# A sequence mixer on one core: state products padded to all 128 rows, projection weight streamed in pieces, norms from one function table, outputs with 128 tokens

## The reference, cut to what matters

```
x = x + mixer(layernorm(x))
x = x + cross_attention(layernorm(x), ctx)
x = x + moe(layernorm(x))
```

```
bc = (value @ W_bc.T).reshape(B, T, 32, 4, 32)        # Bz, Bx, Cz, Cx: 32 states a head
bc = bc / (sqrt(sum(bc*bc, -1)) + 1e-8)
z = S * (z - dt*A*s + dt*Bz*u)                        # per head, state and head channel, step by step
s = s + dt*z + dt*Bx*u
y = Cz . z + Cx . s
out = ((y + skip*value) * silu(gate)) @ W_out.T
```

## Time and profile before

| | |
|---|---|
| median of 3 runs | 3144.58 us (3139.78 to 3146.74) |
| span of the profiled execution | 3057.5 us |
| what lies around the span (median less span) | 87.1 us |
| TensorE busy in the span | 2816.9 us, 92% |
| VectorE busy | 2063.0 us, 67% |
| ScalarE busy | 1286.8 us, 42% |
| DMA | 366.15 MB, mean 120 GB/s |
| 13 units of the mixer, 508.85 to 1899.47 us | 1390.62 us, 106.97 us each |

### The profile page before, as it was taken

One profiled execution on the slowest core, in us unless ns is written; L12 is line 12 of the kernel. 1 busy time (PEld: TensorE's weight loads), 2 busy tenths in 40 slices (PEclk: granted clock), 3 DMA queues, 4 the chain that ended last, 5 costly groups with the idle time before them and its releaser, 6 DMA issues. The chain is left out here.

```text
span 3057.5 us, 83082 instructions
## 1 busy us (share of the span) xinstructions
PE 2816.9 (92%) x34208; PEld 2144.9 (70%) x34208; DVE 2063.0 (67%) x7110; ACT 1286.8 (42%) x2244; POOL 286.6 (9%) x227
## 2 busy tenths in 40 slices
PE   7965999999999999999999999589879999999998
PEld 3434778778877887787788878533335667888887
DVE  7658999999999999898999999555656201111111
ACT  4634545554454554455455545133324222333332
POOL 0000000000000000000000000000000661333344
PEclk9977999999999999999999999779988999999999
DMA  7874354254435424433542542210006332777776
GB/s 270 233 204 113 80 126 108 64 126 112 102 73 129 108 70 116 112 91 83 124 108 58 135 112 76 69 42 1 1 1 253 109 120 87 197 201 197 197 200 181
DMA packets 249233, 366.15 MB, mean 120 GB/s; under 512 B 57771, under 2 KB 172092, under 8 KB 238140
## 3 DMA queue, kind: packets, MB, share of 16 engines
q1 hardware_dynamic: 226428, 335.99, 39.9%
q0 software_dynamic: 22464, 25.31, 3.9%
HBM read 264.99 MB, written 99.84 MB: 119 GB/s over the span
## 5 line engine op out<-in xcount | busy, mean ns | idle before, releaser
L671 PE MATMUL ring<-valt,wbc 128*128 128x256 f32 x4096 | 947.9, 388 | 31.8 <-DMA valt<-valt_scratch 27.7
L671 PEld LDWEIGHTS ring<-valt,wbc 128*128 128x128 f32 x4096 | 777.4, 194 | 169.0 <-issue 61.5
L824 ACT COPY bc<-ring 128x512 f32<-128x512 f32 x256 | 149.5, 584 | 736.4 <-PE ring L671 736.4
L984 DVE TENSOR_TENSOR uu<-phi,coef 128x64 f32<-128x64 f32 x2048 | 355.1, 211 | 2.1
L990 DVE TENSOR_TENSOR phi<-phi,uu 128x64 f32<-128x64 f32 x2048 | 354.5, 211 | 0.1
L2101 DVE TENSOR_SCALAR f_yr<-fp_y,f_meta 128x256 f32<-128x256 f32 x124 | 54.3, 479 | 423.1 <-PE fp_y L1918 423.1
L729 PE MATMUL yp<-bc,hpad 32*32 32x64 f32 x8192 | 260.2, 289 | 5.0 <-DVE hc L1092 5.0
L729 PEld LDWEIGHTS yp<-bc,hpad 32*32 32x32 f32 x8192 | 225.5, 122 | 50.7 <-issue 50.6
L1985 ACT ACTIVATE f_hT<-fp_h,f_b 128x256 f32<-128x256 f32 x248 | 117.4, 473 | 327.3 <-PE fp_h L1909 327.3
L1918 PE MATMUL fp_y<-f_w,f_hT 128*128 128x256 f32 x992 | 230.7, 386 | 7.9
L1909 PE MATMUL fp_h<-f_xrt,f_w 128*128 128x256 f32 x992 | 225.9, 381 | 0.9 <-ACT f_xrt L1974 0.9
(11 more groups left out here) (227 smaller groups left out, 4006.1 us busy)
## 6 DMA issues: line engine op xcount, KB each, us to landing
f_w<-in_W_dram SPq DMA_DIRECT2D x128, 512.0 KB, 4.2
coef<-par_scratch SPq DMA_DIRECT2D x128, 256.0 KB
fb<-fac_scratch SPq DMA_DIRECT2D x256, 128.0 KB, 3.4
fc<-fac_scratch SPq DMA_DIRECT2D x256, 128.0 KB, 3.8
xg_scratch<-f_fill SPq DMA_DIRECT2D x16, 1032.0 KB, 17.5
f_xr<-xg_scratch SPq DMA_DIRECT2D x64, 258.0 KB, 4.9
vtok_scratch<-p_vtok SPq DMA_DIRECT2D x32, 512.0 KB, 7.9
dub<-vtok_scratch SPq DMA_DIRECT2D x16, 1024.0 KB, 7.3
```

Of the source, the lines that this page charges most:

```text
L671: mm = pe.matmul(ring[:, p % 2, v * UT:(v + 1) * UT], wbc[:, k, g, first + v, :], valt[:, u % 2, k, :], start=(k == 0), stop=(k == 3))
L824: nc.scalar.copy(bc[:, gp, first:first + 2, i // 2, :], o).then_inc(bc_ready, 1)
L984: made[k] = mark(V.tensor_tensor(uu[:, k].rearrange("p i (g b) -> p i g b", b=B), phi[:, t, ::-1, k, :].rearrange("p i (g b) -> p i g b", ...
```

## The change

Five edits, all in the mixer and its weight.

1. **State products.** `hpad` becomes an operand with all 128 rows for each j: ScalarE writes it four times (once for each j), scaled by a mask `own` that leaves only head j's 32 rows. `mixed_states` takes all 128 rows of both operands; its outputs stay 32 columns each at the same place of `yp`.
2. **Weight.** `wbc` (64 KB a partition) is gone. A ring `wring` of 4 pieces of 512 KB (a piece is what one `projected` call needs) takes its place. Four pieces are loaded at the start; after that, ScalarE's queue issues the next load into a slot right after the square (L827) that frees it: 252 loads of 512 KB, 16 in a unit, where one load of 8 MB stood.
3. **Norms.** The square root becomes Exp(0.5 Ln(x + 1e-30)), so that each call of `norms` has two Ln and two Exp and no Sqrt; a function table with both is loaded once ahead of the mixer's work.
4. **Outputs.** `outputs` takes 128 tokens at once: the half loop r is gone, 8 products of 128 x 128 with 256 moving columns where there were 16 of 128 x 64. Tokens of `xs` stand in another order, so `load_x` and `store_x` have 4 DMAs of 32 partitions instead of 2 of 64.
5. One more constant (`own`) is loaded, and one tile (`tiny`) is set.

```diff
-            sp.dma_start(wbc[:], d["W_bc"].rearrange("(k p) (g c o) -> p k g c o", p=P, g=G, c=4)).then_inc(wbc_in, 16)
+            for p in range(WRING):
+                sp.dma_start(wring[:, p], d["W_bc"][p]).then_inc(wbc_in, 16)
...
+WPIECES = 4 * GP
+WRING = 4
...
-        hpad = sb("hpad", [P, 2, 2, B, 2 * DH])
+        hpad = sb("hpad", [P, J, DH + 4 * B * 2 * DH])
+        own = sb("own", [P, J])
...
             def store_x(u):
                 sp.wait_ge(x1_ready, u + 1)
-                for r in range(2):
-                    sp.dma_start(x1v[u, r], xs[L * r:L * r + L]).then_inc(x_out, 16)
+                for b in range(B):
+                    sp.dma_start(x1v[u, b], xs[b::B]).then_inc(x_out, 16)
...
             def projected(u, gp, i):                       # TensorE
+                if p >= WRING:
+                    pe.wait_ge(piece_in[p % WRING], 16 * (p // WRING))
...
-                        mm = pe.matmul(ring[:, p % 2, v * UT:(v + 1) * UT], wbc[:, k, g, first + v, :], valt[:, u % 2, k, :],
+                        mm = pe.matmul(ring[:, p % 2, v * UT:(v + 1) * UT], wring[:, p % WRING, k, v, :], valt[:, u % 2, k, :],
...
             def mixed_states(u, gp, more, un, gn):
-                pe.wait_ge(hpad_ready, 2 * n + 2)
+                pe.wait_ge(hpad_ready, J * n + J)
...
+                            k = DH * (2 * ((2 * v + i) * B + b) + 1 - i)
                             for j in range(J):
-                                r = slice(N * j, N * j + N)
-                                pe.matmul(yp[r, b * L:(b + 1) * L], hpad[r, v, i, b, :],
-                                          turns(bc[r, gp, 2 + v, i, :])[:, :, b],
+                                pe.matmul(yp[N * j:N * j + N, b * L:(b + 1) * L], hpad[:, j, k:k + 2 * DH],
+                                          turns(bc[:, gp, 2 + v, i, :])[:, :, b],
...
                 for q in range(2):
-                    for r in range(2):
-                        for k in range(4):
-                            mm = pe.matmul(yp[L * r:L * r + L, q * DM:(q + 1) * DM],
-                                           turns(sg[:, k, :])[:, :, 2 * q + r], wout[:, k, :],
+                    for k in range(4):
+                        mm = pe.matmul(yp[:, q * DM:(q + 1) * DM], sg[:, k, q * P:(q + 1) * P], wout[:, k, :],
...
+            nc.scalar.preload_act_table_set("natural_log_exp_and_others")
...
             def projected(u, gp, i):                       # ScalarE
                 nc.scalar.activation(sq[:, p % 2], o, ACT.Square).then_inc(sq_ready, 1)
+                if p + WRING < WPIECES * NU:
+                    act.dma_start(wring[:, p % WRING], d["W_bc"][(p + WRING) % WPIECES]) \
+                        .then_inc(piece_in[p % WRING], 16)
...
-                nc.scalar.activation(nr[:], ssp[:, 0:UT], ACT.Sqrt).then_inc(nr_root, 1)
+                nc.scalar.activation(nr[:], ssp[:, 0:UT], ACT.Ln, bias=tiny[:, 0:1]).then_inc(nr_square, 1)
+                act.wait_ge(nr_square, n + 1)
+                nc.scalar.activation(nr[:], nr[:], ACT.Exp, scale=0.5).then_inc(nr_root, 1)
...
-                for i in range(2):
-                    nc.scalar.copy(hpad[:, :, i, :, i * DH:(i + 1) * DH], hc[:, gp, :, i]).then_inc(hpad_ready, 1)
+                h = hc[:, gp].rearrange("p v i b e -> p (v i b) e")
+                for j in range(J):
+                    nc.scalar.activation(hpad[:, j, DH:].rearrange("p (x e) -> p x e", e=2 * DH)[:, :, 0:DH], h,
+                                         ACT.Copy, scale=own[:, j:j + 1]).then_inc(hpad_ready, 1)
```

More of the change, by code:

```diff
@@ L28 @@
 EPS_LN, EPS_BC = 1e-5, 1e-8
+SMALLEST = 1e-30
 DT_MIN, DT_MAX, Y_MAX = 1e-4, 0.1, 0.106
@@ L48, in constants @@
     hn = jn[:, None] * G + np.arange(G)[None]
+    c["own"] = (jn[:, None] == np.arange(J)[None]).astype(np.float32)
     c["sel"] = (hn[:, :, None] == np.arange(H)[None, None]).astype(np.float32)
@@ L90, with projections @@
 PIDX = {k: i for i, k in enumerate(PRING)}
-def projections(nc, d, x, st, wbc):
+def projections(nc, d, x, st, wring):
     with ExitStack() as ctx:
@@ L198, in _ @@
             sp.wait_ge(raw_out, 32 * NPASS)
-            sp.wait_ge(wbc_in, 16)
+            sp.wait_ge(wbc_in, 16 * WRING)
         @block.tensor
@@ L401, with mixer @@
 UQ = NU // B
-def mixer(nc, d, st, wbc, x, x1):
+WPIECES = 4 * GP
+WRING = 4
+def mixer(nc, d, st, wring, x, x1):
     with ExitStack() as ctx:
@@ L425, in mixer @@
         epsb = sb("epsb", [P, 1])
+        tiny = sb("tiny", [P, 1])
         phi = sb("phi", [P, L + 1, 2, 2, LANES])
@@ L463, in mixer @@
         w_loaded = sem("w_loaded")
-        NW = 7
+        NW = 8
         set_ready = sem("set_ready")
@@ L481, in mixer @@
         sums_done = sem("sums_done")
+        piece_in = [sem(f"piece_in{i}") for i in range(WRING)]
+        nr_square = sem("nr_square")
         nr_root = sem("nr_root")
@@ L506, in turns @@
             return v.rearrange("p (t b) -> p t b", b=B)
-        xv = x.rearrange("(q r u s) m -> u r s q m", q=2, r=2, s=L)
-        x1v = x1.rearrange("(q r u s) m -> u r s q m", q=2, r=2, s=L)
+        xv = x.rearrange("(b u q t) m -> u b t q m", b=B, q=2, t=L // 2)
+        x1v = x1.rearrange("(b u q t) m -> u b t q m", b=B, q=2, t=L // 2)
         def par(u, q):
@@ L552, in load_x @@
             def load_x(u):
-                for r in range(2):
-                    sp.dma_start(xs[L * r:L * r + L], xv[u, r]).then_inc(x_in, 16)
+                for b in range(B):
+                    sp.dma_start(xs[b::B], xv[u, b]).then_inc(x_in, 16)
             def store_x(u):
                 sp.wait_ge(x1_ready, u + 1)
-                for r in range(2):
-                    sp.dma_start(x1v[u, r], xs[L * r:L * r + L]).then_inc(x_out, 16)
+                for b in range(B):
+                    sp.dma_start(x1v[u, b], xs[b::B]).then_inc(x_out, 16)
             def store_factors(n):
@@ L587, in _ @@
                     (nega[:], d["A_states"]), (sel[:], d["sel"]), (ident[:], d["ident"]), (causal[:], d["causal"]),
-                    (resetm[:], d["resetm"]), (skip[:], d["skip"]),
+                    (resetm[:], d["resetm"]), (skip[:], d["skip"]), (own[:], d["own"]),
                     (wout[:], d["W_out"].rearrange("(k p) o -> p k o", p=P))):
@@ L642, in _ @@
                 if u > 0:
-                    sp.wait_ge(x_out, 32 * u)
+                    sp.wait_ge(x_out, 16 * B * u)
                     load_x(u)
@@ L652, in _ @@
             store_x(NU - 1)
-            sp.wait_ge(x_out, 32 * NU)
+            sp.wait_ge(x_out, 16 * B * NU)
         @block.tensor
@@ L663, in projected @@
                 p = 4 * n + i
-                g, first = 2 * gp + i // 2, 2 * (i % 2)
                 if gp == 0 and i == 0:
                     pe.wait_ge(valt_in, 16 * (u + 1))
+                if p >= WRING:
+                    pe.wait_ge(piece_in[p % WRING], 16 * (p // WRING))
                 if p >= 2:
@@ L680, in summed @@
                 if half == 0 and n > 0:
-                    pe.wait_ge(nr_root, n)
+                    pe.wait_ge(nr_square, n)
                 for i in range(2):
@@ L755, in outputs @@
                 for q in range(2):
-                    for r in range(2):
-                        for k in range(4):
-                            mm = pe.matmul(yp[L * r:L * r + L, q * DM:(q + 1) * DM],
-                                           turns(sg[:, k, :])[:, :, 2 * q + r], wout[:, k, :],
-                                           start=(k == 0), stop=(k == 3), skip_group_check=True)
+                    for k in range(4):
+                        mm = pe.matmul(yp[:, q * DM:(q + 1) * DM], sg[:, k, q * P:(q + 1) * P], wout[:, k, :],
+                                       start=(k == 0), stop=(k == 3), skip_group_check=True)
                 mm.then_inc(o_full, 1)
@@ L926, in _ @@
             V.memset(hpad[:], 0.0)
+            V.memset(tiny[:], SMALLEST)
             V.memset(one[:], 1.0).then_inc(set_ready, 1)
@@ L1097, in residual @@
                 dve.wait_ge(o_full, u + 1)
-                dve.wait_ge(x_in, 32 * (u + 1))
+                dve.wait_ge(x_in, 16 * B * (u + 1))
                 V.tensor_tensor(xs[:], yp[:].rearrange("p (q m) -> p q m", q=2), xs[:], ALU.add).then_inc(x1_ready, 1)
@@ L1154, in attention @@
         ("valt", (NU, P, 4, UT), F32), ("par", (UQ, 5, P, UT), F32), ("fac", (NU * GP, P, UT), F32))}
-    with nc.sbuf_tensor("wbc", [P, 4, G, 4, P], F32) as wbc:
-        projections(nc, d, x, st, wbc)
-        mixer(nc, d, st, wbc, x, x1)
+    with nc.sbuf_tensor("wring", [P, WRING, 4, 2, P], F32) as wring:
+        projections(nc, d, x, st, wring)
+        mixer(nc, d, st, wring, x, x1)
 SK, DC = 77, 192
@@ L2129, in layouts @@
     w = np.asarray(inputs["L0_attn_W_bc"]).reshape(G, J, 4, N, DI)[..., chan]
-    r["W_bc"] = w.transpose(0, 2, 1, 3, 4).reshape(H * 4 * N, DI).T
+    w = w.transpose(0, 2, 1, 3, 4).reshape(WPIECES, 2, P, 4, P)
+    r["W_bc"] = w.transpose(0, 4, 3, 1, 2)
```

## The result

| | before | after |
|---|---|---|
| median, 4 runs each | 3142.76 us (3139.78 to 3146.74) | 3225.48 us (3218.91 to 3231.91) |
| ratio | | 1.025, 95% interval 1.0226 to 1.0275: slower |

The account below looks back on a forecast made before the run. VectorE was taken as the bound: 101.3 us of work a unit plus 5.6 of waits. Terms 15 x (5.4 - 5.6) = -3, +2, +0.5, -4, +0.9 gave -3.6, so 3141 us, range 3116 to 3188.

Parts of the forecast that it names:

- The streamed weight: Mixer: 16 pieces a unit share the DMA engines with the factors; two `fb` waits of 5.4 us together a unit.
- rival 2: Streamed weight makes the factors late, `fb` waits together above 6.0 us a unit: 3180 us (3151 to 3200), chance 0.27.
- First `fb` wait: VectorE's wait for reloaded factors ahead of `inputs(u,2)`: two pieces delay the load, 2.7 us a unit, upper bound 3.8.
- Second wait: VectorE's wait for `fb` of `inputs(u,3)`: 3.2 less 1.0 plus 0.5, so 2.7 us a unit, upper bound 4.4.
- The first recurrence: Mixer's start: two pieces meet the parameters' store ahead of VectorE's first recurrence step, +2 us (0 to 3.3).
- State products: TensorE in each group: padded products fall from 30.1 to 19.0 ns, 5.7 us a unit; lower bound nothing saved.
- Rival 3: Padded state products are no faster, so about 1.0 us a unit of late waits stays: +15, 3156 us, chance 0.06.
- outputs: TensorE's outputs in each unit: 16 instructions at 232 ns, from 4.87 to 3.7 us, 1.15 saved a unit.
- the last store: Mixer's end: the last store has two more DMA issues, +0.9 us.
- At the end: TensorE on the path: state products 1.4 us shorter each, last outputs 6.41 to about 4.9, together -4 us.
- Norms: ScalarE: table loads go, chain to the factors 2.9 us shorter, removing VectorE's 10.5 us of waits in 13 units.
- The frame: Profiled span lay 87.1 us below the runs' median; the sum is a difference on that execution, added to the median.

Follow-up runs that it names:

- e5_turned: The kernel after, with read_out's last two VectorE instructions writing in the order in which TensorE reads, so without a step: ratio 1.0293.
- e8_early_turned: e7_early with the turned write of e5_turned: 3137.53 us, ratio 0.9962 to the kernel before.
- e2_resident: The kernel after with the whole weight resident in SBUF and the state products of before: 3140.35 us, ratio 0.9985 to before.
- e11_after_oldstate: The kernel after, weight still streamed, with the state products of before: 3236.36 us, ratio 1.0265 to before.
- e3_stream_only: The kernel before with the weight streamed and nothing else changed: 3261.22 us, ratio 1.034.
- e7_early: e2_resident with factors(n0+3) scaled, stored and loaded earlier, and the first coefficient set and coefs(u+1) later: 3115.01 us, ratio 0.9898 to before.
- e10_before_early: The kernel before with only the order moves of e7_early, keeping its longer norms and old outputs: 3170.07 us, ratio 1.007.
- e4_half_pieces: The kernel after with half the bytes loaded for each streamed piece, as many transfers: 3168.75 us, ratio 1.0058 to before.
- e6_shifted: The kernel after with a ring of 8 pieces and none issued in a unit's first group: 3176.37 us, ratio 1.0082 to before.
- experiment 5: The kernel before, unchanged, profiled a second time: span 3154.1 us in an execution of 3155.91, against a span of 3057.5 in the first profile.

## Why the prediction was wrong

**The streamed weight** is the step that failed. That its pieces would meet the factors of `inputs(u,2)` was its mechanism, and rival 2 its case against itself, with a chance of 0.27. The price of a piece was right too: 1.63 us of all DMA engines forecast, 1.65 measured (23.5% of 1453.2 us for 207 pieces in the DMA view of after). The size of the waits was wrong, in these terms.
- First `fb` wait: 2.7 a unit (bound 3.8); measured 4.7. The sum put two pieces ahead of the `fb` load alone. But the store of the factors runs through the same crowd ahead of the load: it landed 3.8 us later than before in the mean (9.2 against 5.4), and the load added 1.1 (8.0 against 6.8). The trip to DRAM and back was priced on one of its two legs, and the cost was mostly on the other.
- Second wait: 2.7 (bound 4.4), a fall of 0.3; measured 4.6, a rise of 1.6. The forecast took 1.0 off because the store takes "3.5 us now". That row is one unit; the mean from store to load was 2.9 before and is 2.8 in after, so there was next to nothing to take off. The load leg rose by 1.4 (5.3 to 6.7), where the sum had 0.5: in the unit shown the next piece was issued at 1116.60, beside the load of 1115.40.
- `fc`: put at nothing without a reason; measured 0.8.
- The first recurrence: +2 us (bound 3.3). The wait went from 12.64 to 18.49, but VectorE came to it earlier, and the step itself began 2.5 us later than in the first profile of before and 3.9 later than in the second (243.81 and 242.42, against 246.35). This term was small and nearly right.

The measured waits are 10.4 us a unit (135.2 / 13), where the sum had 5.4 and its upper bound 8.2. Over 15 units the 5.0 us between them are 75 us, most of the 84 us by which the forecast missed.

Two readings of the prediction were wrong beside this. The rows name one coefficient set, that of 1042.08, ahead of the full stretch of 1046 to 1052; the second was issued only at 1059.13. And rival 2's own sum, 3144.6 with +39, +2, +0.5, -4 and +0.9, is 3183 and not 3180. Neither changes the outcome.

**State products**: the bound "nothing saved" was the truth. 19.0 ns came from `mixed_values`, which reads without a step; the text named the step and set it aside because `causal_products` reads with it at 18.0. `e5_turned` and `e8_early_turned` show that the step costs these products half their time in either shape: 32.4 and 31.9 ns with it, 17.0 and 17.2 without. The causal products gain only 6% from the same write (123.0 to 115.6 us in 13 units). Why the step is nearly free there isn't shown. So the comparison in which the prediction saw the rule of banks at work was misread: the 30.1 and 18.0 ns came of how the two kinds of product bear the step, and not of one bank against four. Rival 3's outcome holds, but not its price of +15 us in this kernel: VectorE waits for the factors, and TensorE wasn't late (4.0 us of late masks in 13 units). The Trainium skill, "TensorE: Matmul & The Clock Gate", section "Why this matters for your kernels", says that one product with 32 rows takes as long as one with 128; the trace agrees in both layouts. The Trainium skill, "TensorEngine Tiling (Array Packing)", section Restrictions and Gotchas, states that different row tiles cannot use one PSUM bank at the same time; no cost of that is seen here, since four row groups of one bank run at 17.2 ns, no slower than the 17.4 of causal products with a bank each (115.6 / 6656).

**Right**: VectorE's own work, 101.4 us a unit, in every kernel but the two turned ones (101.3 forecast); outputs, 3.65 us (3.7); norms without table loads, their wait gone; late waits nearly gone; `hpad` and the piece issues hidden on ScalarE; the last store, +0.85 us (VectorE's wait at the mixer's end 3.56 and 4.41). At the end -2.6 us of the -4: the last state products didn't shrink (3.91 and 4.06), the last outputs did (6.41 and 5.41; forecast 4.9).

**Norms**: that the waits for norms would vanish was right, that 0.8 us a unit would come back for it wasn't, even without the stream (`e2_resident`). Together with the outputs they are worth something where TensorE is late (`e11_after_oldstate` against `e3_stream_only`) and once the order is changed with them (`e7_early` against `e10_before_early`).

**The frame**: 87.1 us "around" the span were not time outside the span. The profiled execution was shorter behind the mixer than the others. It cost the forecast nothing, since it was a difference, but a second profile would have told.

**Open**: why half the bytes cost so much less than half (`e4_half_pieces`); and what makes TensorE's instruction packets late. Its nameless wait at L749 is 69.9 us in after, 41.6 in `e4_half_pieces`, 32.0 in `e6_shifted`, and 3.5 for the same instruction in `e2_resident`, so it moves with the stream. In after it can't cost much, since VectorE hardly waits for TensorE. Whether the order of `e7_early` and a ring that keeps the pieces out of group 0 (`e6_shifted`) would together make the streamed kernel fast wasn't run.

## What to carry to other kernels

A mean DMA share of 0.41 leaves room for bytes, not for latency: before streaming a resident operand, find the round trips through DRAM on the critical engine's path, and price the new traffic on each leg of them, store and load, from means over many units and not from one row. When a chain gets shorter, nothing is gained until its consumer, and the queue behind that, are moved to where it now ends. To price a matmul by a neighbour in the trace, match the step of its moving operand as well as its shape; and when a profiled span and the run's time differ by more than a few us, take a second profile.

## What the runs showed of the hardware that was not expected

- A moving operand with a step of 4 elements (16 bytes) doubled the time of 64-column state products, 17 to 32 ns each, whether they use 32 or 128 rows; causal products lost 6%.
- The same step on VectorE's output raised a 128x512 addition from 681 ns to between 1056 and 1067.
- With the weight streamed, TensorE stood up to 5.5 us at a time with no engine named, in all 69.9 us in 13 units at one line of the kernel against 5.4; in 19 of its 22 such waits of over 1 us, at all lines, it went on 1.2 to 1.8 us after a 16 KB packet of instructions had landed. After it stood so from 1103.9 to 1108.0, with the DMA engines at a share of 1.10, its granted clock in the next 6 us was 0.55 of full speed, most of that time at the lower of its two levels (1.2 of 2.4 GHz):

```profile
1108.00:1114.00 6.00, 4.93 (x75) 4.39 (x76) 6.00 (x11) 0.00 (x0) 0.00 (x0) 0.55 0.90 210
```

- In two executions of the same kernel, TensorE ran at the full clock through GpSimd's scatters in one and stood through most of them in the other, 96 us apart (experiment 5).
